# Attention scores with dense q rows as weights and zero-padded k rows moving; row buffers by use, cleared by DMA

## The chip, the core and the metric

The kernel is one program on one core of a Trainium2 chip. A core has five engines that each run their own instruction stream and meet only through semaphores: TensorE (PE in the profile, with its weight loads shown apart as PEld), VectorE (DVE), ScalarE (ACT), GpSimd (POOL) and SyncE (SP), which here does nothing but start DMA transfers and wait. Data lies in SBUF (128 partitions) and in PSUM (here eight banks of 128 partitions by 512 float32 numbers), which TensorE writes. The core has 16 DMA engines, shared by all its transfers.

The metric is the device time of one execution in microseconds (us). The kernel before has a median of 473.09 us over three runs, 469.32 to 474.57.

## The reference, cut to what matters

The input x is 16 sequences of 256 tokens of width 128, float32. Three layers follow each other, each on normalised input and added to x: a mixture of eight experts (two chosen per token), a causal attention, and the same mixture of experts again. The change concerns the attention alone:

```python
q = (x @ Wq).reshape(b, n, h, hd).transpose(0, 2, 1, 3)      # 16 heads of width 8
k = (x @ Wk).reshape(b, n, h, hd).transpose(0, 2, 1, 3)
c = jnp.cumsum(jax.nn.log_sigmoid(x @ Wf).transpose(0, 2, 1), axis=-1)
scores = jnp.einsum('bhid,bhjd->bhij', q, k) * scale
scores = scores + c[..., :, None] - c[..., None, :]
scores = jnp.where(causal, scores, NEG)
attn = jax.nn.softmax(scores, axis=-1)
out = jnp.einsum('bhij,bhjd->bhid', attn, v)
```

## The kernel before, in words

**Layers.** The first mixture of experts runs over groups of 4 token tiles (128 tokens each), the attention over 16 sequences of 2 token tiles, and the second mixture over groups again. `run_layers` writes the order of every compute engine's work out: groups of the first mixture, two steps in which the last groups alternate with the first two attention steps (`beside`), the attention steps 0 to 14, three steps beside the second mixture, and the rest. An attention step has six parts, and in it three sequences are in flight: sequence s has its scores and row maxima made, sequence s-1 its weights (exponentials) and most of the product with v, sequence s-2 its end and output projection, while sequence s+2 gets its q, k and c.

**Scores are computed twice.** First directly, tokens of q on the partitions (`scores`), only for the maximum of each row, which DVE takes out of PSUM (`row_max`). Then turned, tokens of k on the partitions and with the negated maximum added (`turned_scores`); ACT takes the exponential, POOL clears what lies over the diagonal (`causal`), and `times_v` multiplies with v.

**Rows of q and k.** q, k and c are each split in two parts of lower precision. One matmul over 104 contraction rows adds the products: 4 groups of heads (`NG`) times 26 rows (`ROWS`, 8 dimensions in three combinations of parts, and two rows for c) make `KR` = 104. Rows 104 and 105 carry the maximum, rows 106 to 108 a mask, so that `KD` = 109. A q buffer (`q_rows`) holds 16 heads by 256 tokens in each of 109 partitions, 16 KB a partition. A head fills only the rows of its own group and has zeros in the other three groups' rows. A k buffer (`k_rows`) holds 4 columns of heads (`NU`) by 256 tokens and is dense: its 104 rows belong to all four groups. Because q is zero-padded, one k block serves four heads.

**Direct scores before.** For the first token tile (t = 0) each score bank takes four matmuls of 128 columns, one for each head, with the head's q as the weights and k as the moving operand, and one of 512 columns that adds the causal mask. For the second tile (t = 1) each bank takes two matmuls of 256 columns and a mask of 256 columns. There are 4 banks' worth for t = 0 (parts 0 and 1 of the step) and 8 for t = 1 (parts 2 to 5). Two banks alternate: `scores(p)` waits for `row_max(p-2)`.

**How rows are made.** SP (`sync`) runs one step for each sequence: it stores the split parts of q, k and c of sequence s+2 to DRAM (`q_stage`, `k_stage`) and loads the rows of sequence s+1 back in the order above, 4 transfers into `q_rows` and 1 into `k_rows`. There are three buffers of each. ACT sends the maxima into rows 104 and 105 of `q_rows` (`send_max`).

**Set-up of the rows.** The zeros of the three q buffers are written once: two by POOL memsets (`set_up_rows`), one by an ACT copy (`zero_rows`). SP's `constant_rows` waits for them and then writes the constant rows (ones and the mask rows) by small transfers, before it enters `sync`:

```python
def constant_rows(sp):
    sp.wait_ge(zeroed, 4)
```

The memsets on POOL and the copy on ACT stand between instructions of the first two groups of the first mixture. `q_parts` and `k_parts` are single buffers: ACT writes those of the next sequence only when the stores of the one before have landed (`at_least(act, q_stored, ...)`), and TensorE starts step 0 only after `ones_in` and the rows of sequence 0.

Of the kernel before, what the change touches and what calls it, by code (L numbers as in the profile page):

```python
# [4 lines left out]
FP32 = mybir.dt.float32  # L5
FP32R = mybir.dt.float32r
BF16 = mybir.dt.bfloat16
U32 = mybir.dt.uint32
# [38 lines left out]
def run_layers(eng, moe1, attention, moe2, groups, seqs, after=None):  # L47
# [17 lines left out]
    run_steps(eng, lambda i, s: [attention(i, s, k) for k in range(6)], 0, seqs - 1, (2, 2 + (seqs - 5) // 3 * 3), 3)  # L65
# [400 lines left out]
def attention_layer(nc, ctx, c, made, banks, x_all, S_LEN, before):  # L466
# [78 lines left out]
    rows_in = sem("rows_in")  # L545
# [14 lines left out]
    q_dram = nc.dram_tensor("q_stage", (3, 3 * HD, NG, NU, N), FP32, kind="Internal").ap()  # L560
    k_dram = nc.dram_tensor("k_stage", (3, ROWS, NG, NU, N), FP32, kind="Internal").ap()
# [4 lines left out]

    def constant_rows(sp):
# [7 lines left out]
        for b in range(3):  # L575
# [3 lines left out]
                         .broadcast_to([3, NU, N])).then_inc(ones_in, 16)  # L579

    def sync(sp):
        def step(i, s):
            if 0 <= s + 1 < NSEQ:
                b, n = (s + 1) % 3, i + 2
                if 0 <= s:
                    wait_apart(sp, scores_ready, i * 12 + 1, sp_waited)
                at_least(sp, wt_ready, (i - 1) * 12)
                sp.wait_ge(q_stored, n * 16 * 3)
                for g in range(NG):
                    sp.dma_start(raw(q_rows[b])[g:NG * 3 * HD:NG, NU * g:NU * (g + 1), :],  # L590
                                 q_dram[b, :, g]).then_inc(rows_in, 16)
                wait_apart(sp, k_stored, n * 16 * 3, sp_waited)
                sp.wait_ge(c_stored, n * 16 * 2)
                sp.dma_start(raw(k_rows[b])[0:KR, :, :], k_dram[b].rearrange("r g u n -> (r g) u n")).then_inc(rows_in, 16)
            if 0 <= s + 2 < NSEQ:
                b, n = (s + 2) % 3, i + 3
                sp.wait_ge(qk_lo_done, n * 2)
                for r, part in enumerate((0, 1, 0)):
                    sp.dma_start(k_dram[b, r * HD:(r + 1) * HD].rearrange("d g u n -> (d g u) n"),
                                 raw(k_parts)[:, part, :]).then_inc(k_stored, 16)  # L600
                for r, part in enumerate((0, 0, 1)):
                    sp.dma_start(q_dram[b, r * HD:(r + 1) * HD].rearrange("d g u n -> (d g u) n"),
                                 raw(q_parts)[:, part, :]).then_inc(q_stored, 16)
                sp.wait_ge(c_lo_done, n)
                for part in range(2):
                    sp.dma_start(k_dram[b, 3 * HD + part].rearrange("g u n -> (g u) n"), raw(c_parts)[:, part, :]).then_inc(c_stored, 16)
# [492 lines left out]
```

## Time and profile before

| | |
|---|---|
| median of three runs | 473.09 us (469.32 to 474.57) |
| profiled execution, its own time | 470.08 us |
| its span in the trace | 468.3 us |
| busy, share of the span | PE 88%, DVE 79%, ACT 59%, POOL 51% |
| mean granted TensorE clock | 0.983 of full speed |
| DMA packets and bytes | 31905, 32.57 MB |
| by layer (from the lines' own times) | first mixture to about 106 us, attention to about 370 us, second mixture after it |

How to read it: busy time of PE is modelled and matmuls overlap, so the length of a matmul in a list is its latency, several hundred ns even where the next one starts 100 ns later. What a matmul costs in a row of them is read from the starts, or from the chain of waits, which gives each piece only the time that it adds. An instruction that starts a DMA is not counted as busy; SPq and ACTq are the queues' own rows, with the time that the issue took. The DMA share of a window is the mean over the 16 engines, so that 1/16 = 0.06 is one engine busy all the time.

### The profile page before, as it was taken

The page shows a single profiled execution, that of the slowest core. Times are in us where ns is not written, and L with a number is a line of the kernel's source. Part 1 is how long each engine was busy: PE and PEld are TensorE (multiplying, and loading weights), DVE is VectorE, ACT ScalarE, POOL GpSimd, SP SyncE. Part 2 cuts the span into 40 slices and gives each one's busy share as a digit, 9 for nine tenths or more (in the row PEclk, how much of TensorE's full clock was granted, in tenths as well). Part 3 has the DMA queues.
Part 4 walks back from the last instruction along what each step waited for, and adds up shares of the span by engine and source line. Part 5 has one row for each costly group of instructions (what it writes and reads, how often), then busy time and mean ns, then how long its engine had stood idle before and what let it go on. Part 6 is the DMA issues. An engine that isn't in the chain of part 4 may idle for free.

```text
span 468.3 us, 11951 instructions
## 1 busy us (share of the span) xinstructions
PE 412.9 (88%) x3488; PEld 304.2 (65%) x3488; DVE 367.6 (79%) x1316; ACT 277.5 (59%) x758; POOL 239.6 (51%) x397
## 2 busy tenths in 40 slices
PE   0888888766799999999999999999999898888884
PEld 0666666545677777777777777777777566665662
DVE  4999999986866786687678678767757458999995
ACT  4667676451265566557466566655666657667653
POOL 8965556552335544544545454454444425665554
PEclk9999999998889999999999999999999989999999
DMA  3311000043324332322423233242430000001001
GB/s 112 94 54 23 1 0 1 0 140 99 124 81 130 99 116 77 120 94 83 131 82 118 86 112 101 76 142 84 126 84 4 3 3 0 24 26 43 22 22 45
DMA packets 31905, 32.57 MB, mean 70 GB/s; under 512 B 4808, under 2 KB 28636, under 8 KB 31866
## 3 DMA queue, kind: packets, MB, share of 16 engines
q1 hardware_dynamic: 29818, 31.58, 22.1%
q10 hardware_dynamic: 2048, 0.53, 0.6%
q8 instruction: 18, 0.29, 0.3%
q14 instruction: 21, 0.17, 0.1%
HBM read 16.05 MB, written 15.20 MB: 67 GB/s over the span
## 4 chain that ended last, share of the span: by engine, by line
PE 55%; DVE 24%; issue 10%; POOL 5%; ACT 3%; DVEq 1%; DMA 1%; ACTq 1%; POOLq 0%
PE bank L867 14%; PE bank L897 11%; PE bank L882 10%; DVE m_lower L288 7%; PE bank L870 6%; POOL m_pair L216 2%; DVE x_all L297 2%; PE bank L988 2%; DVE m_best_no L376 2%; DVE m_stats L335 2%; PE bank L983 2%; PE bank L940 2%; PE bank L906 1%; PE bank L980 1%; POOL m_upper L220 1%
## 5 line engine op out<-in xcount | busy, mean ns | idle before, releaser
L779 DVE TENSOR_REDUCE a_neg_max<-bank 128x2 f32<-128x512 f32 (+1 forms) x192 | 124.1, 685 | 67.6 <-PE bank L870 66.7
L718 ACT ACTIVATE a_weights<-bank 128x512 f32<-128x512 f32 x192 | 106.7, 591 | 47.6 <-PE bank L882 27.6
L658 POOL TENSOR_SCALAR_AFFINE_SELECT a_weights<-a_weights 128x512 f32<-128x512 f32 (+1 forms) x96 | 75.5, 787 | 112.3 <-ACT a_weights L718 112.3
L867 PE MATMUL bank<-a_k_rows,a_q_rows 104*128 104x256 f32 (+1 forms) x512 | 100.2, 321 | 5.8 <-DVE a_neg_max L779 4.7
L867 PEld LDWEIGHTS bank<-a_k_rows,a_q_rows 104*128 104x128 f32 x512 | 79.0, 198 | 24.6 <-issue 14.4
L246 ACT ACTIVATE m_scaled<-bank,m_gates 128x128 f32<-128x128 f32 x256 | 72.3, 365 | 25.1 <-PE bank L417 25.1
L216 POOL TENSOR_TENSOR m_pair<-m_scaled 128x256 f32<-128x256 f32 x64 | 48.2, 753 | 59.2 <-ACT m_scaled L246 59.1
L882 PE MATMUL bank<-a_q_rows,a_k_rows 106*128 106x512 f32 (+1 forms) x192 | 71.0, 450 | 1.9 <-ACT a_weights L718 1.9
L288 DVE SCALAR_TENSOR_TENSOR m_lower<-bank,m_gates,m_lower 128x128 f32<-128x128 f32 x192 | 65.5, 341 | 1.2
L870 PE MATMUL bank<-a_mask,a_ident 128*128 128x256 bf16 (+1 forms) x192 | 62.9, 327 | 0.0
L897 PE MATMUL bank<-a_weights,a_v 128*32 128x128 f32 x1536 | 62.1, 280 | 0.0
L897 PEld LDWEIGHTS bank<-a_weights,a_v 128*32 128x32 f32 x1536 | 36.4, 110 | 25.5 <-issue 24.4
L416 PE MATMUL bank<-we_hi,m_xt_hi 128*128 128x512 f32 x64 | 31.8, 496 | 15.2 <-DVE m_lower L288 15.1
L705 ACT ACTIVATE a_max_t<-bank 32x128 fp32r<-32x128 f32 x32 | 8.5, 266 | 47.2 <-PE bank L911 47.2
L882 PEld LDWEIGHTS bank<-a_q_rows,a_k_rows 106*128 106x128 f32 (+1 forms) x192 | 30.6, 197 | 5.8 <-ACT a_weights L718 3.3
L220 POOL TENSOR_TENSOR m_upper<-m_pair 128x128 f32<-128x128 f32 x64 | 29.5, 462 | 5.7 <-POOL m_pair L216 1.3
L416 PEld LDWEIGHTS bank<-we_hi,m_xt_hi 128*128 128x128 f32 x64 | 12.1, 190 | 26.6 <-DVE m_lower L288 26.0
L270 ACT ACTIVATE m_xn<-x_all,m_shift,m_rstd 128x128 f32<-128x128 f32 (+1 forms) x64 | 26.3, 483 | 0.2 <-POOL m_shift L228 0.2
L417 PE MATMUL bank<-we_lo,m_xt_hi 128*128 128x512 f32 x64 | 25.6, 399 | 0.0
L417 PE MATMUL bank<-we_hi,m_xt_hi 128*128 128x512 f32 x64 | 25.6, 399 | 0.0
L416 PE MATMUL bank<-we_lo,m_xt_hi 128*128 128x512 f32 x64 | 25.5, 399 | 0.0
L416 PE MATMUL bank<-we_hi,m_xt_lo 128*128 128x512 f32 x64 | 25.4, 398 | 0.0
(126 smaller groups left out, 781.0 us busy)
## 6 DMA issues: line engine op xcount, KB each, us to landing
a_k_rows<-k_stage SPq DMA_DIRECT2D x16, 416.0 KB
k_stage<-a_k_parts SPq DMA_DIRECT2D x48, 128.0 KB, 1.8
q_stage<-a_q_parts SPq DMA_DIRECT2D x48, 128.0 KB, 1.8
a_q_rows<-q_stage SPq DMA_DIRECT2D x64, 96.0 KB
x_all<-in_L_attn_x SPq DMA_DIRECT2D x8, 256.0 KB, 2.8
out_x<-x_all SPq DMA_DIRECT2D x8, 256.0 KB, 2.3
a_q_rows<-a_max_t ACTq DMA_DIRECT2D x64, 8.0 KB, 1.9
we<-in_L_ffn_We SPq DMA_DIRECT2D x1, 512.0 KB, 4.1
```

The costliest lines, as they stand in the source:

```text
L216: nc.gpsimd.tensor_tensor(pair[:, q % 2], scaled[:, q % 2, 0:2], scaled[:, q % 2, 2:4], ALU.add).then_inc(pair_done, 1)
L246: last = nc.scalar.activation(scaled[:, q % 2, j], y_high[q % 2][:, j * D:(j + 1) * D], ACT.Copy, scale=gates[:, s % 2, q, 4 + j:5 + j])
L288: nc.vector.scalar_tensor_tensor(out=lower[:, q % 2, j], in0=y_low[q % 2][:, j * D:(j + 1) * D], scalar=gates[:, s % 2, q, j:j + 1], in1=t ...
L416: nc.tensor.matmul(y_low[q % 2][:, :], x_part, w_part[:, 0:H], start=k == 0, stop=k == 2)
L417: last = nc.tensor.matmul(y_high[q % 2][:, :], x_part, w_part[:, H:2 * H], start=k == 0, stop=k == 2)
L658: nc.gpsimd.affine_select(out=diagonal, in_=diagonal, compare_op=ALU.is_ge, fill=0.0, base=0, pattern=[[0, heads.stop - heads.start], [1, P]],
L718: nc.scalar.activation(weights[n // 2 % 3][:, half:half + 4, :].rearrange("p h n -> p (h n)"), wt_bank[n % 2][:, :], ACT.Exp).then_inc(wt_ ...
L779: nc.vector.tensor_reduce(neg_max[:, t, first:first + heads], score_bank[p % 2][:, :].rearrange("p (h n) -> p h n", h=heads), AX.X, ALU.ma ...
L867: nc.tensor.matmul(bank[:, n * keys:(n + 1) * keys], q_rows[b][0:KR, h, t * P:(t + 1) * P], k_rows[b][0:KR, h % NU, 0:keys], start=n == 0, ...
L870: nc.tensor.matmul(own, ident16[:, :], mask16[:, 0:heads, :], start=False, stop=True, skip_group_check=True).then_inc(scores_ready, 1)
L882: nc.tensor.matmul(bank[:, :], k_rows[b][0:rows, u, jt * P:(jt + 1) * P], q_rows[b][0:rows, u:H:NU, t * P:(t + 1) * P], start=True, stop=T ...
L897: last = nc.tensor.matmul(out_bank[t][32 * g:32 * (g + 1), u // 2 * P:(u // 2 + 1) * P], v_sb[b][:, jt * H // 2 + 2 * g + u // 2, u % 2:u ...
```

## The change

Direct scores get row buffers of their own. `q_dense` (104 rows by 4 columns of heads by 256 tokens) is dense and is the weights; `k_heads` (104 rows by 16 heads by 256 tokens) is zero-padded and moves, 512 columns a matmul: four heads' 128 keys, or two heads' 256 keys. So one matmul fills a bank where four or two did, and the mask matmul stays. Heads come in another order in a bank, and `row_max` writes its maxima in that order. The turned scores keep `q_rows` and `k_rows`. All four kinds have two buffers; the DRAM stages and v have four. SP loads for each step 5 transfers of rows for the direct scores of sequence s+1 and then the 5 for the turned scores of sequence s. The zeros of `q_rows` and `k_heads` (four buffers) come from SP, as four transfers from `zero_row`, a tile of 256 zeros a partition, and `constant_rows` waits for them before it goes on. POOL's memsets and ACT's copy are gone; POOL fills `q_dense` with ones instead, two memsets of 1024 elements a partition.

```diff
-    q_rows = [sb(f"q_rows{b}", [KD, H, N], FP32R) for b in range(3)]
-    k_rows = [sb(f"k_rows{b}", [KD, NU, N], FP32R) for b in range(3)]
-    v_sb = [sb(f"v{b}", [P, 2 * H // 2, 3, HW], FP32) for b in range(3)]
+    q_rows = [sb(f"q_rows{b}", [KD, H, N], FP32R) for b in range(2)]
+    k_rows = [sb(f"k_rows{b}", [KD, NU, N], FP32R) for b in range(2)]
+    q_dense = [sb(f"q_dense{b}", [KR, NU, N], FP32R) for b in range(2)]
+    k_heads = [sb(f"k_heads{b}", [KR, H, N], FP32R) for b in range(2)]
+    v_sb = [sb(f"v{b}", [P, 2 * H // 2, 3, HW], FP32) for b in range(4)]
...
     def constant_rows(sp):
-        sp.wait_ge(zeroed, 4)
+        sp.wait_ge(zero_set, 1)
+        for tile in q_rows + k_heads:
+            rows = tile.shape[0]
+            sp.dma_start(raw(tile), zero_row[0:rows, :].unsqueeze(1).broadcast_to([rows, H, N])).then_inc(rows_zeroed, 16)
+        sp.wait_ge(zeroed, 1)
+        sp.wait_ge(rows_zeroed, 16 * 4)
         ones = ones_r[:, :].bitcast(FP32).rearrange("r (u n) -> r u n", u=NU)
-        for b in range(3):
+        for b in range(2):
...
+        sp.wait_ge(dense_set, 2)
+        sp.wait_ge(ones_in, 16 * 2 * (NG + 3))
 
     def sync(sp):
         def step(i, s):
             if 0 <= s + 1 < NSEQ:
-                b, n = (s + 1) % 3, i + 2
+                b, d, n = (s + 1) % 2, (s + 1) % 4, i + 2
                 if 0 <= s:
                     wait_apart(sp, scores_ready, i * 12 + 1, sp_waited)
-                at_least(sp, wt_ready, (i - 1) * 12)
                 sp.wait_ge(q_stored, n * 16 * 3)
+                sp.dma_start(raw(q_dense[b])[0:NG * 3 * HD, :, :],
+                             q_dram[d].rearrange("r g u n -> (r g) u n")).then_inc(direct_in, 16)
+                wait_apart(sp, k_stored, n * 16 * 3, sp_waited)
+                sp.wait_ge(c_stored, n * 16 * 2)
+                for g in range(NG):
+                    sp.dma_start(raw(k_heads[b])[g:KR:NG, NU * g:NU * (g + 1), :],
+                                 k_dram[d, :, g]).then_inc(direct_in, 16)
+            if 0 <= s < NSEQ:
+                b, d = s % 2, s % 4
+                if 0 < s:
+                    sp.wait_ge(wt_ready, (i - 1) * 12 + 1)
                 for g in range(NG):
                     sp.dma_start(raw(q_rows[b])[g:NG * 3 * HD:NG, NU * g:NU * (g + 1), :],
-                                 q_dram[b, :, g]).then_inc(rows_in, 16)
-                wait_apart(sp, k_stored, n * 16 * 3, sp_waited)
-                sp.wait_ge(c_stored, n * 16 * 2)
-                sp.dma_start(raw(k_rows[b])[0:KR, :, :], k_dram[b].rearrange("r g u n -> (r g) u n")).then_inc(rows_in, 16)
+                                 q_dram[d, :, g]).then_inc(rows_in, 16)
+                sp.dma_start(raw(k_rows[b])[0:KR, :, :], k_dram[d].rearrange("r g u n -> (r g) u n")).then_inc(rows_in, 16)
             if 0 <= s + 2 < NSEQ:
-                b, n = (s + 2) % 3, i + 3
+                d, n = (s + 2) % 4, i + 3
+                at_least(sp, rows_in, (i - 1) * 16 * LOADS)
                 sp.wait_ge(qk_lo_done, n * 2)
...
-    def set_up_rows(pool, b):
-
-        nc.gpsimd.memset(q_rows[b][:, :, :].bitcast(U32), 0).then_inc(zeroed, 1)
-
-    def zero_rows(act, b):
-
-        act.wait_ge(zero_set, 1)
-        nc.scalar.activation(q_rows[b][:, :, :], zero_row[0:KD, :].unsqueeze(1).broadcast_to([KD, H, N]),
-                             ACT.Copy).then_inc(zeroed, 1)
+    def set_up_dense(pool):
+
+        for b in range(2):
+            nc.gpsimd.memset(raw(q_dense[b]), 1.0).then_inc(dense_set, 1)
...
     def tensor(pe):
         def scores(i, s, p):
             at_least(pe, max_done, i * 12 + p - 1)
-            b, bank = s % 3, score_bank[p % 2]
-            t, first, heads = (0, 4 * p, 4) if p < 4 else (1, 2 * (p - 4), 2)
+            b, bank = s % 2, score_bank[p % 2]
+            t, u, heads = (0, p, slice(p, H, NU)) if p < 4 else (1, (p - 4) // 2, two_heads(p))
             keys = (t + 1) * P
-            for n in range(heads):
-                h = first + n
-                nc.tensor.matmul(bank[:, n * keys:(n + 1) * keys], q_rows[b][0:KR, h, t * P:(t + 1) * P],
-                                 k_rows[b][0:KR, h % NU, 0:keys], start=n == 0, stop=False, skip_group_check=True)
+            nc.tensor.matmul(bank[:, :], q_dense[b][0:KR, u, t * P:(t + 1) * P], k_heads[b][0:KR, heads, 0:keys],
+                             start=True, stop=False, skip_group_check=True)
+            heads = BANK // keys
             own = bank[:, :].rearrange("p (h n) -> p h n", h=heads)[:, :, keys - P:keys]
             nc.tensor.matmul(own, ident16[:, :], mask16[:, 0:heads, :], start=False, stop=True,
                              skip_group_check=True).then_inc(scores_ready, 1)
...
             if j == 0 and S:
-                pe.wait_ge(rows_in, (i + 1) * 16 * LOADS)
+                pe.wait_ge(direct_in, (i + 1) * 16 * LOADS)
```

SP's stream, at the place between the loads of x and the first stores of q, k and c (a DMA row gives the transfer's shape, partitions first, and how many follow each other):

```order
-L572 DMA a_q_rows<-a_ones_r 2x1024 x4
-L573 DMA a_k_rows<-a_ones_r 2x1024
...
-L576 DMA a_q_rows<-a_later_q 3x16x256
-L578 DMA a_k_rows<-a_later_k 3x4x256
...
+L578 DMA a_q_rows<-a_zero_row 109x16x256 x2
+L578 DMA a_k_heads<-a_zero_row 104x16x256 x2
+L584 DMA a_q_rows<-a_ones_r 2x1024 x4
+L585 DMA a_k_rows<-a_ones_r 2x1024
+L584 DMA a_q_rows<-a_ones_r 2x1024 x4
+L585 DMA a_k_rows<-a_ones_r 2x1024
+L588 DMA a_q_rows<-a_later_q 3x16x256
+L590 DMA a_k_rows<-a_later_k 3x4x256
```

Four large transfers have come ahead of the small ones, which are those of two buffers now and not of three. SP's stream in the loop over sequences, the loads of one step:

```order
+L602 DMA a_q_dense<-q_stage 96x1024
+L605 REGISTER_ALU
+L607 DMA a_k_heads<-k_stage 26x1024 x4
+L612 ISA
+L614 DMA a_q_rows<-q_stage 24x1024 x4
...
-L590 DMA a_q_rows<-q_stage 24x1024 x4
-L593 REGISTER_ALU
-L594 DMA a_k_rows<-k_stage 104x1024
```

Ten loads stand where five did.

## Rows read from the trace of the kernel before

**Rows 1.** The page: PE busy, granted clock and DMA share in 40 slices (11.7 us each).
```profile
PE   0888888766799999999999999999999898888884
PEclk9999999998889999999999999999999989999999
DMA  3311000043324332322423233242430000001001
```

**Rows 2.** Chain of waits, part 5 into part 0: start, us that it adds, work.
```profile
237.32 0.24 PE bank L867 x2
...
237.68 0.46 PE bank L882 x2
...
239.58 0.40 PE bank L867 x4
239.98 0.23 PE bank L870
...
240.84 0.07 issue
```

**Rows 3.** Timeline of DVE, one attention step: start, us, work, idle before.
```profile
232.01 1.29 DVE L779 TENSOR_REDUCE a_neg_max<-bank 128x2 f32<-128x512 f32 x2 [1.31 <-PE bank L870]
...
240.26 0.41 DVE L856 TENSOR_TENSOR x_all<-x_all,bank 128x256 f32 x1
240.70 1.29 DVE L779 TENSOR_REDUCE a_neg_max<-bank 128x4 f32<-128x512 f32 x2
```

**Rows 4.** Timeline of SP's queue (start, us to issue), set-up and first stores.
```profile
28.27 2.54 SPq L572 DMA_DIRECT2D a_q_rows<-a_ones_r  x4
...
43.35 0.70 SPq L578 DMA_DIRECT2D a_k_rows<-a_later_k  x1
94.98 1.33 SPq L599 DMA_DIRECT2D k_stage<-a_k_parts  x3
```

**Rows 5.** SP's waits from 90 to 125 us: total, times, longest.
```profile
SPq L599 <- DVE a_k_parts L841: 62.3, 3, 50.9
```

**Rows 6.** The page: DMA queues with packets, MB, share of 16 engines.
```profile
q1 hardware_dynamic: 29818, 31.58, 22.1%
q10 hardware_dynamic: 2048, 0.53, 0.6%
```

**Rows 7.** Windows: busy by engine, granted clock, then DMA share and GB/s.
```profile
30.00:30.50 0.50, 0.50 (x2) 0.31 (x3) 0.50 (x3) 0.50 (x3) 0.50 (x1) 1.00 0.12 31
43.50:44.00 0.50, 0.38 (x2) 0.34 (x3) 0.50 (x6) 0.00 (x0) 0.42 (x3) 1.00 0.10 23
44.00:45.00 1.00, 1.00 (x6) 0.72 (x4) 1.00 (x12) 0.40 (x2) 0.92 (x2) 1.00 0.16 25
46.50:47.00 0.50, 0.50 (x4) 0.41 (x3) 0.50 (x4) 0.50 (x3) 0.00 (x0) 1.00 0.08 16
104.00:105.00 1.00, 1.00 (x4) 0.68 (x4) 0.16 (x1) 0.00 (x0) 0.92 (x2) 1.00 0.70 270
222.00:223.00 1.00, 1.00 (x22) 0.80 (x14) 0.97 (x3) 0.61 (x2) 0.44 (x2) 1.00 0.77 264
```

**Rows 8.** Timeline of PE: the first direct scores of steps 0 and 1.
```profile
106.29 0.63 PE L867 MATMUL bank<-a_k_rows,a_q_rows 104*128 104x128 f32 x4 [1.16 <-DMA a_k_rows<-k_stage]
...
122.80 0.63 PE L867 MATMUL bank<-a_k_rows,a_q_rows 104*128 104x128 f32 x4 [1.23 <-DVE a_neg_max L779]
```

**Rows 9.** Timeline of SP's queue in one attention step.
```profile
226.77 2.96 SPq L590 DMA_DIRECT2D a_q_rows<-q_stage  x4
229.93 0.38 SPq L594 DMA_DIRECT2D a_k_rows<-k_stage  x1
237.66 1.31 SPq L599 DMA_DIRECT2D k_stage<-a_k_parts  x3
```

**Rows 10.** Timeline of the start: ACT's clearing, and PE's wait behind it.
```profile
10.62 3.61 ACT L616 ACTIVATE a_q_rows<-a_zero_row 109x4096 fp32r<-109x4096 f32 x1
...
15.82 1.11 PE L458 MATMUL bank<-ident,m_xn 128*128 128x128 f32 x4 [1.45 <-ACT m_xn L270]
```

More of the change, by code:

```diff
@@ L64, in run_layers @@
     beside("amamammaaa", -1, moe1, groups - 1)
-    run_steps(eng, lambda i, s: [attention(i, s, k) for k in range(6)], 0, seqs - 1, (2, 2 + (seqs - 5) // 3 * 3), 3)
+    run_steps(eng, lambda i, s: [attention(i, s, k) for k in range(6)], 0, seqs - 1, (2, 2 + (seqs - 5) // 4 * 4), 4)
     beside("amaamamaam", seqs - 1, moe2, -2)
@@ L605, in step @@
                 for part in range(2):
-                    sp.dma_start(k_dram[b, 3 * HD + part].rearrange("g u n -> (g u) n"), raw(c_parts)[:, part, :]).then_inc(c_stored, 16)
-        run_steps(sp, step, -2, NSEQ + 2, (2, 2 + (NSEQ - 4) // 3 * 3), 3)
-    def set_up_rows(pool, b):
-        nc.gpsimd.memset(q_rows[b][:, :, :].bitcast(U32), 0).then_inc(zeroed, 1)
-    def zero_rows(act, b):
-        act.wait_ge(zero_set, 1)
-        nc.scalar.activation(q_rows[b][:, :, :], zero_row[0:KD, :].unsqueeze(1).broadcast_to([KD, H, N]),
-                             ACT.Copy).then_inc(zeroed, 1)
+                    sp.dma_start(k_dram[d, 3 * HD + part].rearrange("g u n -> (g u) n"), raw(c_parts)[:, part, :]).then_inc(c_stored, 16)
+        run_steps(sp, step, -2, NSEQ + 2, (2, 2 + (NSEQ - 4) // 4 * 4), 4)
+    def set_up_dense(pool):
+        for b in range(2):
+            nc.gpsimd.memset(raw(q_dense[b]), 1.0).then_inc(dense_set, 1)
     def set_up_zero(pool):
@@ L622, in set_up_columns @@
     def set_up_columns(pool):
-        for b in range(3):
+        for b in range(4):
             nc.gpsimd.memset(v_sb[b][:, :, :, :], 0.0).then_inc(v_zeroed, 1)
@@ L777, in row_max @@
             dve.wait_ge(scores_ready, i * 12 + p + 1)
-            t, first, heads = (0, 4 * p, 4) if p < 4 else (1, 2 * (p - 4), 2)
-            nc.vector.tensor_reduce(neg_max[:, t, first:first + heads],
-                                    score_bank[p % 2][:, :].rearrange("p (h n) -> p h n", h=heads),
+            t, heads = (0, slice(p, H, NU)) if p < 4 else (1, two_heads(p))
+            nc.vector.tensor_reduce(neg_max[:, t, heads],
+                                    score_bank[p % 2][:, :].rearrange("p (h n) -> p h n", n=(t + 1) * P),
                                     AX.X, ALU.max, negate=True).then_inc(max_done, 1)
@@ L878, in turned_scores @@
             at_least(pe, wt_exp, i * 12 + n - 1)
-            b, bank = s % 3, wt_bank[n % 2]
+            b, bank = s % 2, wt_bank[n % 2]
             t, u, jt = (0, n, 0) if n < 4 else (1, (n - 4) // 2, n % 2)
@@ L892, in times_v @@
                 at_least(pe, attn_done, i * 2)
-            b, w = s % 3, weights[k % 3]
+            b, w = s % 4, weights[k % 3]
             for half in range(2):
@@ L920, in part @@
                 pe.wait_ge(set_up, 2)
-                pe.wait_ge(ones_in, 16 * 3 * (NG + 3))
+                pe.wait_ge(ones_in, 16 * 2 * (NG + 3))
                 pe.wait_ge(before["tiles_done"], 2 * NSEQ)
@@ L991, in tensor @@
         return part
-    return dict(constant_rows=constant_rows, sync=sync, set_up_rows=set_up_rows, zero_rows=zero_rows, set_up_zero=set_up_zero,
+    return dict(constant_rows=constant_rows, sync=sync, set_up_dense=set_up_dense, set_up_zero=set_up_zero,
                 set_up_columns=set_up_columns, set_up_masks=set_up_masks,
@@ L1046, in _ @@
             attention["set_up_zero"](pool)
-            attention["set_up_rows"](pool, 0)
             def after(i):
                 if i == -2:
-                    attention["set_up_rows"](pool, 1)
+                    attention["set_up_dense"](pool)
                     attention["set_up_columns"](pool)
@@ L1061, in after @@
             def after(i):
-                if i == -2:
-                    attention["zero_rows"](act, 2)
                 if i == -1:
```

20 lines of the change are left out of this document (11 added, 9 removed).

## The prediction, made before the changed kernel ran

> **What bounds the kernel now.** First the page's slices [rows 1]. The two mixtures of experts lie at both ends; between about 106 and 370 us, in the attention, PE is at 9 tenths at nearly full clock, and the DMA engines are busy 2 to 4 tenths. From slice 5 to slice 8 (47 to 94 us) they are idle.
>
> Then the chain of waits through one attention step [rows 2]. Nearly every piece is PE's own work. One bank of direct scores for t = 0 adds 0.40 us for its four matmuls and 0.23 for the mask; a second bank for t = 1 adds 0.24 for its two; two turned matmuls of 512 columns add 0.46. Only 0.07 us is a wait, before the transpose of the maxima (L911) in part 0. Its last releaser is seen on DVE [rows 3]: from 232.01 to 242.0 DVE has no idle time that the list marks, through `x_all` at 240.26 + 0.41 = 240.67, for which that transpose waits. So from part 3 to part 0 DVE is as late as PE; before part 3 DVE waited 1.31 us for PE.
>
> Last, SP's queue ahead of the attention [rows 4, 5]. The small constant transfers are issued from 28.27 to 44.05 us. Then SP waits 50.9 us for the q and k of sequence 0 and stores them at 94.98. That is the room for anything that is added to `constant_rows`, and what comes after it is not hidden: TensorE cannot start step 0 before `ones_in` and the rows of sequence 0, and ACT cannot write the parts of sequence 1 before the stores of sequence 0 have landed.
>
> **The clearing, by four transfers.** They move 109 x 16 KB = 1.786 MB twice (`q_rows`) and 104 x 16 KB = 1.704 MB twice (`k_heads`). What matters is on how many DMA engines each one runs. The page counts 29818 packets in SP's queue [rows 6]. The data packets can be counted from the code (a row of 4 KB, 1 KB or 512 B is one packet): stores of q and k 96 x 128, of c 32 x 16; loads 64 x 24 and 16 x 104; x in and out 16 x 512; experts 1024; small weights 768; bias 96; ones 30; mask rows 3 x 48 and 3 x 12. They sum to 26290 and leave 3528. In ACT's queue the same count leaves 2048 - 64 x 16 = 1024 for 64 transfers of 16 rows: 16 each, one for each engine that took part. The 3528 come out exactly if a transfer runs on the largest number of engines up to 16 that divides its rows: 16 for 128, 64 or 16 rows, 13 for 104 rows, 12 for 24, 8, 3 and 2 for 8, 3 and 2 rows, and 4 for Wo, whose DRAM side has 4 blocks (2400 + 16 x 13 + 64 x 12 + 96 + 18 + 30 + 8 = 3528). Fifteen or sixteen engines for 104 rows would give 3560 or 3576. The mask rows, three rows of sixteen 1 KB pieces of one source row, are also seen at 0.10 to 0.16 of the engines [rows 7]. Now 109 is a prime number: **the transfer into `q_rows` gets one engine**, and both get the same one or wait for each other. 104 rows get 13.
>
> The Trainium skill states the same rule (DMA: Bandwidth & Descriptors, "Why a DMA increments its semaphore by 16 and not by 1"): the largest count up to 16 that divides the slowest dimension of both sides, and 1 for 127 partitions. The count above agrees; no run here shows a large prime.
>
> The rate of one engine: 264 GB/s at a share of 0.77 is 21.4 GB/s for a busy engine with 1 KB packets, 270 at 0.70 is 24.1 with 4 KB [rows 7]. Lower bound of time: the mask rows' transfers are the only ones that repeat a source row inside SBUF; they hold 23 to 25 GB/s whether 1.6 engines (0.10) or 2.6 (0.16) are busy. That is one limit shared by neighbouring rows, so a lone engine gets at most 25. Upper bound: two engines at 25 get 12.5 each. I take 22, near the 1 KB stores. Then one `q_rows` takes 81.2 us (71.4 to 143) and one `k_heads` on 13 engines 6.0 us (5.2 to 10.5). The four together: 174.3 us (153 to 307).
>
> They start at 28.3 and their first packet comes 2.0 us later, as for the ones [rows 4, 7]. Behind them 14 small transfers instead of 21: two thirds of 15.8 us is 10.5, and 2.5 for the last to land (traffic ends by 47, 3 us after the last issue) [rows 4, 7]. SP enters `sync` at 28.3 + 2.0 + 174.3 + 13 = 217.6, where it stood ready at 94.98: **+122.6 us**. Nothing covers it: the first mixture ends at 106, and then all engines stand.
>
> **After the stall.** Stores, c, loads follow as before: 11.3 us from the first store to the first scores [rows 4, 8]. The loads now end with four 26-row transfers into `k_heads`, which wait for c, as `k_rows` did; I take no difference. DVE no longer has the last expert group in step 0, and steps 0 to 1 took 16.5 us with waits for DVE [rows 8]; PE on the other hand comes out of 110 us of standing, where before the short stands at its beginning went with granted clock 8 in slices 10 to 12 [rows 1]. Net -3 us (between 0 and -6).
>
> **Direct scores.** For t = 0 a bank's 0.40 us becomes one 512-column matmul, 0.46/2 = 0.23: 0.17 less, four times a step, two in part 0 and two in part 1. For t = 1, 0.24 against 0.23: nothing. Of the 0.68 a step, the half in part 0 comes ahead of the transpose that waits for DVE's `x_all` [rows 2, 3], and DVE has no more time there: it turns into a wait. The other half lies where DVE waits for PE [rows 3] and is kept: 0.33 us in 14 steps, -4.6 us (-9 if DVE gave way). DVE's maxima read 512 columns as before, 0.65 each.
>
> **Loads.** A step of 16.5 us issues 3.3 us of loads and now some 3.4 more (one of 0.38, four of 0.74) [rows 9]. They start at 226.8 and end by 233.5; the stores come at 237.7. The new 0.8 MB need 3.1 us at 264 GB/s. The direct rows land some 6 us before the next step, the turned rows some 4 us before. Hidden. Two buffers instead of three wait for the first turned matmul of the step (just after part 0's scores), before SP is there. If this cover went, each step would wait for the landing; SP's 3.4 us are the price.
>
> **Start.** ACT's copy of 3.61 us is gone; PE waited 1.45 for the work behind it [rows 10]. POOL loses two memsets and gains three short pairs. -1.2 us.
>
> **Sum**, on the profiled execution's 470.1 us: +122.6 - 3 - 4.6 - 1.2 = **584 us**. The median of the runs shown is 473.1, 3 us above that execution, no more than the rounding of this sum. With the bounds for one engine: 25 GB/s gives 153 us, so 563; 12.5 gives 307 us, so 717.
>
> **Rivals.**
>
> 1. *The clearing spreads and is hidden* (faster). If 109 rows went as seven to an engine, each `q_rows` would take 112 KB / 22 GB/s = 5 us, the four some 22 us, against 50.9 of room. The end would be 470.1 - 4.6 - 1.2 - 0.3 = 464. It decides from about 20 us a transfer, that is from four engines on. For it: every large transfer seen runs at 264 to 270 GB/s. Against it: the count of 3528. The same page of the skill has a rule for it ("Measured"): transfers of 1 MB and more reach 78% of peak, 341 GB/s; by it each transfer would take 5 us, and the time would be that 464. I give it 0.08.
> 2. *One engine, but it reads and writes at half the rate*, as two busy engines had it. 640 to 720. For it: reading and writing the same partition's side of SBUF in 1 KB pieces is what the slow transfers did. Against it: that limit was shared by three. 0.22.
> 3. *Clearing hidden, gain lost too*: DVE bound everywhere, or the doubled loads delay the maxima's way into `q_rows` by some tenths a step. 467 to 473, no change. 0.05.
>
> My forecast, one engine at 20 to 25 GB/s, has 0.65: 560 to 640. The range 555 to 720 leaves out the rivals 1 and 3 and little more. One per cent of this kernel is about what its measurement can tell from no change. Faster by more than that 0.07, within it 0.06, slower 0.87.
>
> **What would show it.** In the changed kernel's timeline SP issues `a_q_rows<-a_zero_row` near 28 us and its first store near 218 instead of 95; in the windows between, the DMA share is 0.06 (one of 16) at 20 to 25 GB/s, except some 6 us twice at up to 0.81; all compute engines are idle from about 106 to 225. The completion packets of both `q_rows` transfers are one each. In the attention the step is 16.2 us, with the wait before the transpose of the maxima in part 0 at 0.3 to 0.4 us. I am wrong if the share is far above 0.06 while the clearing runs, or if SP enters the stores at 95 as before; then rival 1 stands. A share of 0.06 at 12 GB/s is rival 2.

## The result, and the profile of the changed kernel

The changed kernel takes 589.79 us (median of four runs, 587.77 to 590.46) against 473.44 us before (469.32 to 474.57, measured with it): 1.247 times as long, with a 95% interval of 1.241 to 1.253. The forecast was 584. Some executions of a kernel run slower as a whole, at a lower granted clock; the ratios here leave them out, the medians and ranges do not.

The page first: PE's busy tenths, the granted clock and the DMA share in 40 slices of 14.7 us, then SP's queue and the chain of waits.

```profile
PE   2888876000000000799999999999999999988885
...
PEclk9999999655555555889999999999999999999998
DMA  4210000000002714555645454555554530001011
...
q1 hardware_dynamic: 40864, 51.57, 30.1%
...
SPq L578 27%; PE bank L883 7%; PE bank L915 6%; PE bank L900 6%; DMA a_k_heads<-a_zero_row 4%; PE bank L887 3%; DMA x_all<-in_L_attn_x 3%; DVE a_neg_max L797 3%; DVE m_lower L288 2%; ACT a_weights L736 1%; POOL m_pair L216 1%; ACTq L728 1%;
```

Where [rows 1] had the attention begin, PE now has nine slices of nothing (slices 8 to 16). Through slices 4 to 12 the DMA engines show 0 tenths although a transfer is running all that time: it runs on one engine of sixteen. The chain of work that ended last gives 27% of the span to L578, the line that issues the clearing.

SP's queue, to be set beside [rows 4]: start, us to issue, what; and its wait for the clearing (total, times, longest).

```profile
28.32 77.39 SPq L578 DMA_DIRECT2D a_q_rows<-a_zero_row  x2
105.75 87.77 SPq L578 DMA_DIRECT2D a_k_heads<-a_zero_row  x2
211.10 2.54 SPq L584 DMA_DIRECT2D a_q_rows<-a_ones_r  x4
...
220.42 0.70 SPq L590 DMA_DIRECT2D a_k_rows<-a_later_k  x1
224.34 1.33 SPq L622 DMA_DIRECT2D k_stage<-a_k_parts  x3
```
```profile
SPq L580 <- DMA a_k_heads<-a_zero_row: 17.5, 1, 17.5
```

The first store comes at 224.34 instead of 94.98. Issuing itself takes 77 and 88 us here. The first `q_rows` is issued in 0.82 us, and the next two issues take nearly a transfer each:

```profile
29.17 76.53 SPq L578 DMA_DIRECT2D a_q_rows<-a_zero_row  x1
105.75 79.92 SPq L578 DMA_DIRECT2D a_k_heads<-a_zero_row  x1
```

Both of these issues end, at 105.7 and 185.7 us, when 112 of the 1744 packets of 1 KB of the `q_rows` transfer in front have yet to start (counted in the packed trace). That is how it would look if the one engine's queue held about that many packets and SP stood in the middle of an issue until there was room; this explanation is inferred, not tested.

Windows in the stretch of clearing (the last three numbers are granted clock, DMA share, GB/s), to be set beside [rows 7]:

```profile
40.00:90.00 50.00, 41.70 (x203) 30.79 (x202) 49.14 (x256) 32.06 (x110) 29.01 (x49) 1.00 0.07 23
...
150.00:180.00 30.00, 0.00 (x0) 0.00 (x0) 0.00 (x0) 0.00 (x0) 0.00 (x0) 0.50 0.07 22
...
195.00:200.00 5.00, 0.00 (x0) 0.00 (x0) 0.00 (x0) 0.00 (x0) 0.00 (x0) 0.50 0.83 177
```
```profile
184.00:186.00 2.00, 0.00 (x0) 0.00 (x0) 0.00 (x0) 0.00 (x0) 0.00 (x0) 0.50 0.07 22
186.00:188.00 2.00, 0.00 (x0) 0.00 (x0) 0.00 (x0) 0.00 (x0) 0.00 (x0) 0.50 0.62 145
...
209.00:210.00 1.00, 0.00 (x0) 0.00 (x0) 0.00 (x0) 0.00 (x0) 0.00 (x0) 0.50 0.07 23
```

Until about 186.3 us one engine of sixteen works at 22 to 23 GB/s. The first packet of the first `q_rows` starts at 30.2 us and its completion packet at 110.9: 80.7 us for one transfer, 22.1 GB/s. (A completion packet is one of 4 bytes that each engine of a transfer sends at its end; the packed trace has its time.) The second `q_rows` ends near 192. The other engines begin with the `k_heads` at 186.3, while that one still has about 100 packets of `q_rows` left, and the last packet ends at 210.5: some 24 us for the two `k_heads`, with the DMA share rising from 0.62 to 0.83 and falling again at the end. While everything stands (from about 108 us on), TensorE's granted clock is 0.50, the lower level.

In the attention: the first direct scores of steps 0 and 1 (beside [rows 8]), then DVE's addition into `x_all` in three steps in a row, and the transposes of the maxima in part 0 behind two of them.

```profile
234.66 1.65 PE L883 MATMUL bank<-a_k_heads,a_q_dense 104*128 104x512 f32 x2 [129.76 <-DMA a_k_heads<-k_stage]
...
248.57 0.47 PE L883 MATMUL bank<-a_k_heads,a_q_dense 104*128 104x512 f32 x1 [1.25 <-DVE a_neg_max L797]
```
```profile
281.02 0.41 DVE L874 TENSOR_TENSOR x_all<-x_all,bank 128x256 f32 x1
298.48 0.41 DVE L874 TENSOR_TENSOR x_all<-x_all,bank 128x256 f32 x1
314.66 0.41 DVE L874 TENSOR_TENSOR x_all<-x_all,bank 128x256 f32 x1
```
```profile
299.12 0.28 PE L929 MATMUL bank<-ident,a_max_parts 128*32 128x128 f32 x1 [0.60 <-DVE x_all L874]
...
315.31 0.28 PE L929 MATMUL bank<-ident,a_max_parts 128*32 128x128 f32 x1 [0.42 <-DVE x_all L874]
```

A step takes about 16.2 us (before: 16.6), from 298.48 on; the first of the two distances above, 17.46 us, belongs to the restart. In most of these steps the transpose waits 0.4 to 0.65 us for `x_all`.

### The profile page after: what moved, and what is told of

It reads as the page before. It is cut to its first block, busy times and chain, and to the rows that moved or that the text cites. A ratio compares the mean times of both kernels' runs of the same rounds, so it can differ in the third digit from the quotient of the medians.

```text
span 588.4 us, 11300 instructions
## 1 busy us (share of the span) xinstructions
PE 403.5 (69%) x3153; PEld 264.7 (45%) x3168; DVE 366.5 (62%) x1316; ACT 273.9 (47%) x757; POOL 235.0 (40%) x399
## 4 chain that ended last, share of the span: by engine, by line
SPq 32%; PE 31%; DVE 12%; DMA 10%; issue 8%; POOL 3%; ACT 2%; ACTq 1%; DVEq 1%; POOLq 0%
SPq L578 27%; PE bank L883 7%; PE bank L915 6%; PE bank L900 6%; DMA a_k_heads<-a_zero_row 4%; PE bank L887 3%; DMA x_all<-in_L_attn_x 3%; DVE a_neg_max L797 3%; DVE m_lower L288 2%; ACT a_weights L736 1%; POOL m_pair L216 1%; ACTq L728 1%; PE bank L958 1%; DMA a_k_rows<-k_stage 1%; PE bank L1001 1%
## 5 line engine op out<-in xcount | busy, mean ns | idle before, releaser
L883 PE MATMUL bank<-a_k_heads,a_q_dense 104*128 104x512 f32 x192 | 89.2, 522 | 131.4 <-DMA a_k_heads<-k_stage 129.8
L883 PEld LDWEIGHTS bank<-a_k_heads,a_q_dense 104*128 104x128 f32 x192 | 38.4, 200 | 148.9 <-issue 142.2
L857 DVE SCALAR_TENSOR_TENSOR a_q_parts<-bank,a_q_parts 128x256 fp32r<-128x256 f32 x16 | 6.7, 416 | 121.4 <-ACT a_k_parts L764 121.4
L763 ACT ACTIVATE a_q_parts<-bank 128x256 fp32r<-128x256 f32 x16 | 6.1, 383 | 128.6 <-DMA q_stage<-a_q_parts 124.9
L707 POOL TENSOR_TENSOR a_c_parts<-a_neg_c,a_zero_row 16x256 fp32r<-16x256 f32 x16 | 11.5, 717 | 127.5 <-DVE a_neg_c L867 127.4
L887 PE MATMUL bank<-a_mask,a_ident 128*128 128x256 bf16 (+1 forms) x177 | 57.0, 322 | 0.0
L887 PEld LDWEIGHTS bank<-a_mask,a_ident 128*128 128x128 bf16 x192 | 19.0, 99 | 35.5 <-issue 27.2
L900 PEld LDWEIGHTS bank<-a_q_rows,a_k_rows 106*128 106x128 f32 (+1 forms) x192 | 30.2, 193 | 8.1 <-ACT a_weights L736 5.2
```

The lines of the kernel that those rows point to most:

```text
L883: nc.tensor.matmul(bank[:, :], q_dense[b][0:KR, u, t * P:(t + 1) * P], k_heads[b][0:KR, heads, 0:keys], start=True, stop=False, skip_group ...
L887: nc.tensor.matmul(own, ident16[:, :], mask16[:, 0:heads, :], start=False, stop=True, skip_group_check=True).then_inc(scores_ready, 1)
L900: nc.tensor.matmul(bank[:, :], k_rows[b][0:rows, u, jt * P:(jt + 1) * P], q_rows[b][0:rows, u:H:NU, t * P:(t + 1) * P], start=True, stop=T ...
```

## The experiments

Ten runs follow; two of them are of the same kernel. All ratios are to the kernel before, measured beside it, with the 95% interval.

### One row count changed: 112 instead of 109

```diff
-    q_rows = [sb(f"q_rows{b}", [KD, H, N], FP32R) for b in range(2)]
+    q_rows = [sb(f"q_rows{b}", [112, H, N], FP32R) for b in range(2)]
```

The clearing takes its rows from the tile's shape, so it writes 112; nothing else in the kernel reads rows 109 to 111.

> The changed kernel with q_rows allocated and cleared over 112 partitions and not 109 (112 = 7 x 16; the three more are never read). Theory (a transfer runs on the largest number of engines up to 16 that divides its rows): the two clearings of q_rows take 16 engines and end within some 9 us each, at the 172 to 177 GB/s that the clearing of k_heads had in the changed kernel; SP is ready for its first store near 80 us and makes it near 95, the stall is gone, and the time is 464 us (462 to 467). Rival (the stall comes from the amount that SP must clear or from its place in the queue, whatever the rows): 585 to 592 as before.

Measured: 463.39 us (461.29 to 466.38), ratio 0.978 (0.970 to 0.987). SP's queue and two windows:

```profile
28.07 3.60 SPq L578 DMA_DIRECT2D a_q_rows<-a_zero_row  x2
31.71 16.85 SPq L578 DMA_DIRECT2D a_k_heads<-a_zero_row  x2
67.45 2.54 SPq L584 DMA_DIRECT2D a_q_rows<-a_ones_r  x4
...
94.92 1.33 SPq L622 DMA_DIRECT2D k_stage<-a_k_parts  x3
```
```profile
31.00:40.00 9.00, 7.57 (x40) 5.76 (x38) 8.96 (x50) 6.04 (x21) 5.17 (x9) 1.00 0.99 250
40.00:50.00 10.00, 8.55 (x43) 6.47 (x42) 9.87 (x54) 6.83 (x24) 5.96 (x11) 1.00 1.02 194
```

Three more rows of zeros take 126 us off. All sixteen engines are busy at 250 GB/s, the first store is at 94.92 as in the kernel before, and SP still waits 17.4 us for q and k in front of it: the clearing is hidden. SP's queue has 40990 packets, 126 more than the changed kernel. Of these, 96 are the data of the added rows (2 transfers, 3 rows, 16 packets of 1 KB), and 30 are left: 2 x (16 - 1) completion packets. So the transfer of 109 rows had one, that of 112 has sixteen. The packed trace shows them: one at 110.9 us in the changed kernel, sixteen between 35.8 and 39.1 us and sixteen more by 47.3 us here. The `k_heads` can be counted too. A version below without any clearing by DMA has 34020 packets in this queue, 6844 fewer than the changed kernel: 6816 are data, and 28 = 2 x 1 + 2 x 13 are completion packets, so the 104 rows had thirteen engines.

### The same transfer cut in two

```diff
-        for tile in q_rows + k_heads:
-            rows = tile.shape[0]
-            sp.dma_start(raw(tile), zero_row[0:rows, :].unsqueeze(1).broadcast_to([rows, H, N])).then_inc(rows_zeroed, 16)
+        for tile, first, last in ((q_rows[0], 0, 106), (q_rows[0], 106, 109), (q_rows[1], 0, 106), (q_rows[1], 106, 109),
+                                  (k_heads[0], 0, 104), (k_heads[1], 0, 104)):
+            sp.dma_start(raw(tile)[first:last], zero_row[first:last, :].unsqueeze(1).broadcast_to([last - first, H, N])).then_inc(rows_zeroed, 16)
```

106 is 2 x 53.

> The changed kernel with each clearing of q_rows split in 106 rows and 3 rows. 106 = 2 x 53. Theory: two engines with 53 rows each, 868 KB at the 22 GB/s that one engine had, 39 us in place of 80; DMA share 0.13 at 44 GB/s while it runs; first store near 145 us, time near 510 us (500 to 520). Rival A (one limit of 25 GB/s that engines share when source and destination lie in SBUF): share 0.13 at 25 GB/s, 70 us a transfer, time near 570. Rival B (rows beyond a size or a number are packed 7 or 8 to an engine unless prime): share over 0.8 and time near 464.

Measured: 510.6 us (509.8 to 511.4), ratio 1.077 (1.067 to 1.087). A window of it:

```profile
60.00:100.00 40.00, 30.76 (x147) 22.62 (x147) 37.97 (x179) 23.52 (x81) 22.63 (x37) 1.00 0.14 45
```

Measured beside the 0.07 and 23 GB/s above, this is twice the share and twice the rate. The packets are 40872, 8 more than with 109 rows at once: 2 x (2 + 3) against 2 x 1. So the time follows the divisor of the row count, and two engines do not share one engine's rate: rivals A and B are both out.

### One such transfer in the kernel before

```diff
...
     def constant_rows(sp):
-        sp.wait_ge(zeroed, 4)
+        sp.wait_ge(zero_set, 1)
+        sp.dma_start(raw(q_rows[2]), zero_row[0:KD, :].unsqueeze(1).broadcast_to([KD, H, N])).then_inc(rows_zeroed, 16)
+        sp.wait_ge(zeroed, 3)
+        sp.wait_ge(rows_zeroed, 16)
...
-                    attention["zero_rows"](act, 2)
```

> The kernel before, with one of its three q buffers cleared by SP with one transfer of 109 rows in place of ACT's copy; nothing else of the change. Theory: 80 us on one engine at a DMA share of 0.06; SP's first store moves from 95 to 28 + 2 + 80 + 19 = 129 us and the time to 473 + 34 = 507 us (502 to 511). Rival (the stall needs the doubled buffers, the loads or the direct rows of the change): 472 to 474.

Measured: 506.43 us (505.77 to 507.09), ratio 1.068 (1.058 to 1.078). SP's queue and a window:

```profile
28.67 0.82 SPq L569 DMA_DIRECT2D a_q_rows<-a_zero_row  x1
111.52 2.51 SPq L575 DMA_DIRECT2D a_q_rows<-a_ones_r  x4
...
127.20 2.73 SPq L602 DMA_DIRECT2D k_stage<-a_k_parts  x3
```
```profile
60.00:100.00 40.00, 30.58 (x147) 22.13 (x145) 38.05 (x180) 23.76 (x84) 22.03 (x37) 1.00 0.07 23
```

The clearing alone, without the direct scores and with none of the other edits, costs its time less the room before the first store. It takes 81 us (30.2 to 111.0), and the first store is 32.2 us later than before. SP's queue has 31563 packets, 1745 more than before: 109 x 16 = 1744 of data and one completion packet.

### The direct scores without any clearing by DMA

Two memsets on POOL clear `q_rows`, two copies on ACT clear `k_heads`:

```diff
-            sp.dma_start(raw(tile), zero_row[0:rows, :].unsqueeze(1).broadcast_to([rows, H, N])).then_inc(rows_zeroed, 16)
...
+        nc.gpsimd.memset(q_rows[b][:, :, :].bitcast(U32), 0).then_inc(rows_zeroed, 1)
...
+        nc.scalar.activation(k_heads[b][:, :, :], zero_row[0:KR, :].unsqueeze(1).broadcast_to([KR, H, N]),
+                             ACT.Copy).then_inc(rows_zeroed, 1)
```

> The changed kernel with no clearing by DMA: two POOL memsets for q_rows and two ACT copies for k_heads, 3.5 to 3.6 us each, where the kernel before had two and one. So this is the change without its new clearing. Theory: 4.6 us less than before in the attention as in the changed kernel, and 2 to 4 us more at the start because ACT clears twice before the second group: 470 us (467 to 472). Against the kernel with clearing over 112 rows it tells what moving the clearing to SP is worth: 3 to 6 us. Rival (direct scores cost nothing less on the whole): 473 to 477.

Measured: 471.12 us (467.55 to 473.98, ten runs), ratio 0.994 (0.990 to 0.998). The start on ACT:

```profile
10.63 7.11 ACT L636 ACTIVATE a_k_heads<-a_zero_row 104x4096 fp32r<-104x4096 f32 x2
17.64 1.64 ACT L270 ACTIVATE m_xn<-x_all,m_shift,m_rstd 128x128 f32<-128x128 f32 x4
```

Two copies of 3.5 us stand ahead of the first mixture's second group of normalized rows: they start at 17.64, and at 10.54 in the version with 112 rows. Most of the gain of the version with 112 rows is lost (471.1 against 463.4). Between the two profiled executions it is 8.1 us. Of these 3.1 lie ahead of the first store (98.05 against 94.92), behind the copies, and 4.1 between the first and the last addition into `x_all`, where no copy stands; the cause of those is open. By the measured times DMA is the better place for the clearing, once the row count is right.

### Loads: is SP's queue the next limit?

In the version with 112 rows, each load of a part of `k_heads` is followed by a second one into a tile that nothing reads:

```diff
                     sp.dma_start(raw(k_heads[b])[g:KR:NG, NU * g:NU * (g + 1), :],
                                  k_dram[d, :, g]).then_inc(direct_in, 16)
+                    sp.dma_start(spare[g:KR:NG, :, :], k_dram[d, :, g]).then_inc(direct_in, 16)
```

> The changed kernel with the q row buffers cleared over 112 partitions, and every load of the padded k rows issued a second time into a spare tile: 14 loads a step instead of 10, with some 1.5 times the bytes. Theory (the loads are hidden: the store of the next step's rows lands long before its scores are due): 463 to 465 us. Rival (the rows on SP's queue are close to being the limit, and the direct scores pay for their larger loads): 466 us or more, growing with the steps.

> The changed kernel with the q row buffers cleared over 112 partitions, on the same chip as the versions above, as their yardstick: 463 us (461 to 466).

Measured: 485.83 us (482.16 to 490.02), ratio 1.029 (1.017 to 1.041), beside 463.78 us (461.46 to 469.53), ratio 0.983 (0.976 to 0.989), for the version without them. My theory fell: 22 us, with some 6 us of uncertainty, for loads that nobody reads. (TensorE's wait at the start of a step counts these loads as well; in the profile they hold it up once, by 3.1 us.) PE's waits from 100 to 430 us, and SP's waits for DVE there (total, times, longest):

```profile
PE bank L902 <- DMA a_k_rows<-k_stage: 13.4, 12, 3.2
```
```profile
SPq L624 <- DVE a_k_parts L861: 6.1, 5, 2.6
```

The same wait of SP in the version without them:

```profile
SPq L622 <- DVE a_k_parts L859: 35.9, 15, 5.7
```

That line is SP's slack: 35.9 / 15 = 2.4 us a step in which it has issued all loads and waits for the next q and k. Four issues of 0.73 us are 2.9. With them SP comes late to the stores, the next loads wait for the stores (11 times, 11.9 us in all), and TensorE for `a_k_rows` (13.4 us of the 22). Two more kernels part the time of issuing from the traffic: four loads of one row each, and one load of 104 rows.

```diff
+                    sp.dma_start(spare[g:g + 1, :, :], k_dram[d, 0:1, g]).then_inc(direct_in, 16)
...
+                sp.dma_start(spare[:, :, :], k_dram[d].rearrange("r g u n -> (r g) u n")).then_inc(direct_in, 16)
```

> As the version with the loads of padded k rows issued twice (485.8 us), but each of the four additional loads of a step moves one row of 4 KB instead of 26. It keeps what SP's queue takes to issue them and takes the traffic away. Theory (the time of issuing in SP's queue, 2.9 us a step ahead of the q rows and k rows, is what delays them): 0.6 us or more for each issue remains, so 478 to 486 us, and TensorE waits for a_k_rows as often as there. Rival (the additional 0.43 MB a step on the DMA engines delay them): 463 to 467 us, as without the additional loads.

> As the version with the loads of padded k rows issued twice (485.8 us), but the additional bytes of a step come in one load of 104 rows instead of four of 26. It keeps the traffic and takes three of the four issues away. Theory (time of issuing): one issue of 0.5 us is left of 2.9, within the 2.2 us of room: 463 to 467 us. Rival (traffic): 478 to 486 us, as with the four.

Measured: 473.36 us (468.81 to 475.84), ratio 1.002 (0.998 to 1.006), for four small loads; 466.61 us (465.23 to 467.96), ratio 0.989 (0.983 to 0.994), for one large. Windows over the same 80 us, small then large:

```profile
180.00:260.00 80.00, 77.31 (x761) 47.17 (x756) 59.27 (x143) 48.58 (x117) 38.48 (x63) 1.00 0.51 154
```
```profile
180.00:260.00 80.00, 76.78 (x766) 47.28 (x769) 59.92 (x144) 48.42 (x117) 39.03 (x63) 1.00 0.58 177
```

By the ratios, against 0.983 without added loads, the large load costs some 3 us (within its uncertainty nothing) although it raises the traffic to 177 GB/s from the 152 without added loads. The four small ones leave the traffic nearly as it was (154) and cost about 9 (0.44 us each to issue, 1.8 a step, less than the average slack), fewer than the 15 to 22 that I expected; TensorE waits for `a_k_rows` 3 times and not 12, 4.1 us in all. So issuing is the larger part; together the two make 12 of the 22 us. That the rest comes from both together, past the slack, is a guess that was not tested.

### DVE's order: x_all before the scan of c

```diff
             if j == 5 and F:
...
-                dve.wait_ge(log_sig_done, n)
-                at_least(dve, c_lo_done, n - 1)
-                nc.vector.tensor_tensor_scan(neg_c[:, :], ones_row[:, :], log_sig[:, :], 0.0,
-                                             ALU.mult, ALU.subtract).then_inc(c_done, 1)
...
                 nc.vector.tensor_tensor(pair, pair, side_bank[:, 0:2 * D], ALU.add).then_inc(proj_added, 1)
+            if j == 5 and F:
+                dve.wait_ge(log_sig_done, n)
+                at_least(dve, c_lo_done, n - 1)
+                nc.vector.tensor_tensor_scan(neg_c[:, :], ones_row[:, :], log_sig[:, :], 0.0,
+                                             ALU.mult, ALU.subtract).then_inc(c_done, 1)
```

In the version with 112 rows:

> The changed kernel with the q row buffers cleared over 112 partitions, and in part 5 DVE's addition of the projection into x_all put ahead of its scan of c. In the version with 112 partitions the first transpose of the maxima waited 0.56 us for x_all. Theory (that wait ends on DVE's order, and the addition is what it waits for): the wait falls to 0 to 0.1 us, a step takes 15.7 to 15.8 us instead of 16.2, and the time is about 457 us, 5 to 7 us below the version with the old order. Rival (DVE's whole sequence of a step sets its length by now, so that moving an instruction within it moves the wait to another place): 463 us, within 1 us of the old order.

In the kernel before:

> The kernel before with the same exchange alone: DVE adds the projection into x_all ahead of its scan of c. There the wait for x_all at the transposes was 0.07 us. Theory (the order matters only where the direct scores have made the path through TensorE shorter): 472 to 474 us, a gain of 1 us at most. Rival (the order is worth 5 us by itself): 468 us.

Measured: 457.9 us (456.36 to 461.57), ratio 0.973 (0.966 to 0.979), on top of the direct scores: 5 to 6 us below the old order (ratio 0.983), as the theory had it, though the two intervals overlap. This version beats both kernels. In the kernel before: 467.5 us (462.64 to 470.09), ratio 0.988 (0.981 to 0.995), a gain of about 6 us (1.2%) where my theory allowed 1. The rival was right.

The cause is seen in starts rather than in the listed idle times. The mask matmul and the transpose of the maxima behind it in part 0, in the kernel before:

```profile
207.25 0.39 PE L870 MATMUL bank<-a_mask,a_ident 128*128 128x512 bf16 x1
207.83 0.28 PE L911 MATMUL bank<-ident,a_max_parts 128*32 128x128 f32 x1 [0.19 <-issue]
```

With DVE's order changed in it:

```profile
210.31 0.39 PE L871 MATMUL bank<-a_mask,a_ident 128*128 128x512 bf16 x1
210.53 0.27 PE L912 MATMUL bank<-ident,a_max_parts 128*32 128x128 f32 x1
```

With 112 rows, old order:

```profile
219.67 0.39 PE L887 MATMUL bank<-a_mask,a_ident 128*128 128x512 bf16 x1
220.62 0.28 PE L929 MATMUL bank<-ident,a_max_parts 128*32 128x128 f32 x1 [0.56 <-DVE x_all L874]
```

With 112 rows, new order:

```profile
218.07 0.39 PE L888 MATMUL bank<-a_mask,a_ident 128*128 128x512 bf16 x1
218.33 0.28 PE L930 MATMUL bank<-ident,a_max_parts 128*32 128x128 f32 x1
```

From start to start it is 0.58 us before and 0.22 with the new order: the kernel before lost 0.36 us in this step, while the list marks 0.19, because the modelled end of the mask's row covers part of the wait. With the direct scores it is 0.95 against 0.26, 0.69 lost where 0.56 is marked.

One step is not the mean, and a step times 14 would mislead. Summed over the last 14 of the 15 steps in each profile, the distance from the mask's start to the transpose's falls by 2.6 us in the kernel before and by 6.4 us with 112 rows; the distance from the mask's start to that of the turned matmul behind the transpose falls by 4.9 and 4.8 us. The stretch from the first to the last addition into `x_all` falls by 6.0 and 4.2 us. So the gain is seen at this place in both kernels; the transpose's own wait is less than half of it in the kernel before, and some 1 us of the gain there is not found.

## Why the prediction was right

**The clearing on one engine: right, and this is the time.** The same kernel with 112 rows takes 463 us, with 109 it takes 590. The share, the rate, the completion packets and the time of the two-engine version all follow the rule of the largest divisor, read from the count of 3528 [rows 6]. The Trainium skill's rule (DMA: Bandwidth & Descriptors, "Why a DMA increments its semaphore by 16 and not by 1") is now shown here at 109 rows (one engine) and at 112 (sixteen). Rival 1 is false for 109 rows. The figure of 341 GB/s that stood beside it is, in the Trainium skill (DMA: Bandwidth & Descriptors, "Measured"), one for loads from HBM into 128 partitions issued from GpSimd, so it did not speak for this transfer. The 109 rows went at 22 GB/s here. Rival 2, one engine at half the rate, is false by the same 22 GB/s, and rival 3 fails for the clearing that is hidden, since 463 us is a gain.

The sum of rival 1, 464, is what 112 rows give (463.4), but that is partly luck. The sum forecast 6.1 us less than one execution of 470.1; measured are 10.5 us less than the median beside it, and 7.3 between the two profiled executions.

**Its size: the lone engine right, the thirteen wrong.** One `q_rows` took 80.7 us, 22.1 GB/s; I had taken 22 GB/s and 81.2 us. The mis-sized term is that of the `k_heads`: the two took 24 us instead of 12. I had given thirteen engines thirteen times the rate of one, 286 GB/s; the windows show 177 at most, and 3.41 MB in 24 us is 142. Some 6 of these 24 us were spent beside the end of the second `q_rows`. So all four took 180.3 us (30.2 to 210.5) instead of 174.3, and these 6.0 us are most of the 6.7 by which the first store came later than forecast (224.3 against 217.6). The range of the term, up to 10.5 us for one `k_heads`, did not hold it.

**The base: some luck in the last digits.** The sum stood on one execution of 470.1 us, and I called its distance to the median no more than rounding. From profile to profile the span grew by 120.1 us (468.3 to 588.4), where the sum had 113.8. From median to median the time grew by 116.3, because the profiled execution of the kernel before was 3.4 us faster than its median and that of the changed one was near it. So part of the error in the `k_heads` does not show in 589.8 against 584.

**The bound from the mask rows was argued wrongly.** I read their 23 to 25 GB/s [rows 7] as one limit that neighbouring rows share, and took a lone engine's ceiling and the lower rate of rival 2 from it. Two engines on 53 rows each reached 45 GB/s. The ceiling of 25 held, but not for that reason; why the mask rows' transfers are slow stays open.

**After the stall: right.** From the first store to the end of the span it was 373.3 us before and is 364.1 now, 9.2 less; forecast 7.6 (3.0 and 4.6). The parts: up to the first addition into `x_all` 62.2 became 56.7; from there to the last 234.9 became 230.8 (384.37 - 154.81 = 229.6 with 112 rows); from the last to the end 76.2 became 76.6. With 112 rows, where nothing stalls, the first part takes 59.9 us. So 3.2 of its 5.5 us came with the stall, for the 3 that I had put there, and the other 2.3 did not need it. The kernel before with one transfer of 109 rows also stalls, for 32 us, and there the first part is 65.3 us, 3 longer than without. Why a stall shortens the restart in one kernel and lengthens it in the other is open.

**Direct scores: the term is right, the wait is not.** In most of the attention a step became 0.35 to 0.4 us shorter (0.33 forecast), in all 4.1 us of the 4.6, and TensorE's wait before the transpose is mostly 0.4 to 0.65 us as listed, not 0.3 to 0.4. I had read 0.07 us of waiting there before [rows 2], in one step and from ends that are modelled; start to start it was 0.19 us on the mean of 14 steps (2.6 / 14) and 0.35 up to the turned matmul (4.9 / 14). "-9 if DVE gave way" was half right: with DVE's order changed in both kernels, a step went from 16.11 to 15.66 us, 0.45 instead of 0.66. With 112 rows 0.49 us lie between the start of the mask matmul and that of the first turned matmul (218.07 to 218.56), in the kernel before 0.25 (210.31 to 210.56), and most steps look like these two. The trace names no releaser, so this 0.2 us is open.

**Loads: hidden, with less room than forecast.** In the changed kernel's attention TensorE waits for `a_k_rows` once, 0.9 us, but the slack is 2.4 us a step in SP's queue, where I had written of some 4 before the rows are due. I had named SP's 3.4 us as the price if the cover went. With 2.9 us more issued, 22 us in some 15 steps were lost, 1.5 a step.

**Start: not shown either way.** With ACT's copy gone, ACT's next rows start at 10.54 us instead of 14.13 in the version with 112 rows, yet the first store there is at 94.92 against 94.98. The other undisturbed profiles with this start have it at 93.27 to 94.83 us (four of them), and the kernel before with DVE's order changed has it at 96.41. The five are 1.7 us earlier on the mean than the two, in the direction of the 1.2 us forecast, but a single kernel's profiles scatter as much.

## What to carry to other kernels

Before a large DMA is written, factor the number of its rows. A prime above 16, or twice such a prime, puts megabytes on one or two engines (seen here at 109 and at 106 rows), and three rows of padding were worth a fifth of the run time. To see how many engines a transfer used, count its completion packets, and look for a steady share of 1/16 or 2/16 in the windows: in the page's tenths that reads as 0. Where a change shortens one engine's path, read the wait behind it from starts and not from listed idle time, over all steps and not from one, and then move what that engine waits for ahead of what nobody waits for.

## What the runs showed that I had not expected

- An engine in these copies from SBUF to SBUF in 1 KB pieces is slower when many are at work: 22 GB/s alone, 45 / 2 = 22.5 with two, 250 / (0.99 x 16) = 15.8 with sixteen, 177 / (0.83 x 16) = 13.3 at the best with thirteen. Over the whole 24 us the last is 3.41 MB / 24 us / 13 = 10.9, with a tail in which one engine works alone (0.07, 23 GB/s). In the version with 112 rows, the windows fell from 250 GB/s (31 to 40 us) to 169 (50 to 60 us) when the clearing went on from sixteen engines to thirteen (the last completion packet of `q_rows` is at 47.3 us). Since thirteen are slower than sixteen, their number is not the whole cause. Why was not tested.
- An issue can take as long as the transfer ahead of it: two issues of `a_q_rows<-a_zero_row` took 77.39 us with one engine, 3.60 with sixteen. A single one, in the kernel before, took 0.82 us.
- Four loads a step that nobody reads cost 22 us, with the DMA engines busy 0.58 of the time (172 GB/s). One load of about the same bytes, at 0.58 and 177 GB/s, cost some 3: so what ran out first was not the engines' time but that in which SP's queue can issue, 0.73 us for each of the four.
